# Four residual layers on one core: LayerNorm 1 kept by feature, its variance from a product with ones, its result added onto x in DRAM

## What is computed

```python
# layer 0, per token; D = 2 traces
ctx    = causal_ema(x, tau_ctx)
wg     = sigmoid([x, ctx] @ Wg.T + bg);  gated = x * wg
mod    = 0.5 + sigmoid(gelu(x @ Wn1.T + bn1) @ Wn2.T + bn2)
traces = causal_ema(gated * mod[d], tau[d])         # d = 0, 1
temporal = sum_d traces[d] * softmax(blend)[d]
gate   = sigmoid(temporal @ Wtemp.T + btemp)
soma   = gelu(x @ Wsoma.T + bsoma)
out    = (soma * gate) @ Wout.T
x = x + (out - mean(out)) / sqrt(var(out) + 1e-5) * gamma + beta   # LayerNorm 1
# layer 1: x = x + x @ W1[cat] + b1[cat]
# layer 2: h = relu(x @ A[lang] + a[lang]) @ B[lang] + b2[lang];  x = x + LayerNorm2(x + h)
# layer 3: x = x + x @ W3[subj].T + b3[subj]
```

## Time and profile before

| | |
|---|---|
| median of 3 runs | 786.71 us (786.17 to 790.17) |
| the profiled execution | 787.42 us |
| its span | 785.6 us |
| PE busy | 767.6 us (98%) |
| DVE busy | 533.8 us (68%) |
| ACT busy | 323.8 us (41%) |
| POOL busy | 101.4 us (13%) |
| HBM read, written | 40.67 MB, 25.20 MB |
| granted TensorE clock | full in every slice of the span |

### The profile page before, as it was taken

How to read it: one execution, slowest core, us unless ns; L and a number is a source line. 1 busy time by engine, 2 the same in 40 slices (tenths; PEclk the granted TensorE clock), 3 DMA queues, 4 the chain that set the end, 5 groups by cost and what they waited for, 6 DMA issues and landing times. The chain is left out here.

```text
span 785.6 us, 10804 instructions
## 1 busy us (share of the span) xinstructions
PE 767.6 (98%) x3628; PEld 628.3 (80%) x3628; DVE 533.8 (68%) x782; ACT 323.8 (41%) x525; POOL 101.4 (13%) x227
## 2 busy tenths in 40 slices
PE   5999999999999999999999999998999999999997
PEld 4888888888888888888888888776888888888885
DVE  3598894694695595595596587746775776657645
ACT  4444426226225315315325424656453544535332
POOL 2000020021012003003003004324001020110110
PEclk9999999999999999999999999999999999999999
DMA  7413004004004004102102514443142241313102
GB/s 222 167 55 108 27 1 161 28 0 161 27 0 160 27 0 146 41 0 111 76 0 81 136 53 157 146 146 141 41 148 70 105 147 41 121 63 111 40 28 82
DMA packets 32480, 66.29 MB, mean 84 GB/s; under 512 B 10800, under 2 KB 11824, under 8 KB 30400
## 3 DMA queue, kind: packets, MB, share of 16 engines
q1 hardware_dynamic: 32224, 65.87, 24.2%
q0 software_dynamic: 224, 0.00, 0.0%
HBM read 40.67 MB, written 25.20 MB: 84 GB/s over the span
## 5 line engine op out<-in xcount | busy, mean ns | idle before, releaser
L557 PE MATMUL pc<-x_h,wg_h 128*128 128x512 f32 x224 | 89.2, 398 | 0.0
L559 PE MATMUL pc<-x_h,wg_l 128*128 128x512 f32 x224 | 88.0, 393 | 0.0
L558 PE MATMUL pc<-x_l,wg_h 128*128 128x512 f32 x224 | 87.2, 389 | 0.0
L1292 DVE TENSOR_TENSOR_SCAN stage_b<-alpha,carry,stage_b 128x512 f32<-128x512 f32 x64 | 78.4, 1267 | 0.0
L999 ACT ACTIVATE ctx_t<-ctx_t,col_bg 128x512 f32<-128x512 f32 x32 | 23.2, 724 | 97.4 <-DVE ctx_t L1272 97.4
L1227 DVE TENSOR_TENSOR x_l<-x_t,x_h 128x512 fp32r<-128x512 f32 x32 | 22.2, 692 | 47.5 <-ACT x_t L949 47.5
L653 PE MATMUL pm<-t_h,wt_h 128*128 128x512 f32 x128 | 51.4, 402 | 0.0
L557 PE MATMUL pm<-wo_h,s_h 128*128 128x512 f32 x128 | 50.6, 395 | 0.7 <-DVE s_l L1251 0.7
L559 PE MATMUL pm<-wo_h,s_l 128*128 128x512 f32 x128 | 50.5, 394 | 0.0
L558 PE MATMUL pm<-wo_l,s_h 128*128 128x512 f32 x128 | 50.4, 394 | 0.0
L655 PE MATMUL pm<-t_h,wt_l 128*128 128x512 f32 x128 | 50.3, 393 | 0.0
(11 more groups left out here) (226 smaller groups left out, 1881.1 us busy)
## 6 DMA issues: line engine op xcount, KB each, us to landing
xt_scratch<-x_t SPq DMA_DIRECT2D x8, 1024.0 KB, 4.0
n_scratch<-stage_a SPq DMA_DIRECT2D x8, 1024.0 KB, 4.7
ctx_t<-xt_scratch SPq DMA_DIRECT2D x16, 512.0 KB, 6.4
x_tok<-in_x_dram SPq DMA_DIRECT2D x30, 256.0 KB, 2.8
out_dram<-x_tok SPq DMA_DIRECT2D x28, 256.0 KB, 2.0
s_h<-n_scratch SPq DMA_DIRECT2D x12, 512.0 KB, 4.9
mod<-mod_scratch SPq DMA_DIRECT2D x8, 512.0 KB, 3.5
stage_b<-in_L_cond_weight_dram SPq DMA_DIRECT2D x2, 1024.0 KB, 5.5
```

The costliest lines, as they stand in the source:

```text
L557: nc.tensor.matmul(acc, ah, bh, start=start and q == 0, stop=False)
L558: nc.tensor.matmul(acc, ah, bl, start=False, stop=False)
L559: last = nc.tensor.matmul(acc, al, bh, start=False, stop=stop and q == n - 1)
L1292: nc.vector.tensor_tensor_scan(tr[:, m % 2, :], alpha[:, 1 + d:2 + d].to_broadcast([P, BLK]), tr[:, m % 2, :], carry[:, D - d, m:m + 1], A ...
```

## The change

LayerNorm 1 is made by feature instead of by token, and its result is added onto x in DRAM.

- Wout is centred over its outputs when it is prepared: each turned quarter of it gets its row mean subtracted (centre_wout: bn_stats, bn_aggr and a negation on DVE; ACT's copy takes the negated mean as its bias, DVE's low part too). The mean of out over the features is then zero and is never computed. The factor 0.5 goes; the variance gets 4 * eps in its place.
- out_chunk(j, m) has Wout as weights and gives out by feature in pm[m].
- The variance over the features: ACT squares the four chunks into stage_a (square), DVE adds them up (add_squares, eps added in the last), ACT and DVE split the sum (squares_hi, squares_lo), PE multiplies it with a 128x128 matrix of 1/512 into pt[0] (variance, two matmuls), which gives the variance of each token on all partitions. DVE takes the reciprocal (inverse), ACT its root (root), and DVE's normalise1 makes gamma * out * rstd from pm[m] into stage_a.
- POOL's add_x1(j) issues one DMA with an add: stage_a onto block j of xt_scratch. store_n, the n loads, turn_y and y_sum_part are gone; load_y loads the sum, by feature. Blocks 2 and later wait for all eight of these stores.
- step_end alternates out_chunk(i-1, m) with v_chunk(i, m), puts variance(i-1) behind soma_chunk(i, 0), and the queues of ACT and DVE are ordered anew. norm1_scale leaves POOL.

```diff
+        ss_h, ss_l = h_h[:, :], h_l[:, :]
+        ones = c_h[:, NC - 1, 0:P]
+        rstd1 = gate[:, 0, :]
+        wo_mean = sb("wo_mean", [P, NC])
 ...
-            def store_n(j):
-                sp.wait_ge(ln_out, j * TILES + TILES)
-                sp.dma_start(block_of(n_scratch, j), stage_a[:, :, :]).then_inc(n_out, 16)
 ...
             def load_y(i):
 
-                sp.wait_ge(ty_done, i * NC)
-                sp.wait_ge(n_out, i * 16 + 16)
-                for half in range(2):
-                    load_n_half(i, s_h[:, 2 * half:2 * half + 2, :].bitcast(F32), half)
+                sp.wait_ge(x1_out, (i * 16 + 16) if isinstance(i, int) and i < 2 else NBLK * 16)
                 sp.wait_ge(y_lo, i * NC)
                 for half in range(2):
-                    load_xt_half(i, half)
+                    load_y_half(i, half)
 ...
+            def add_x1(j):
+
+                pool.wait_ge(xt_out, j * 16 + 16)
+                pool.wait_ge(ln_out, j * NC + NC)
+                pool.dma_start(block_of(xt_scratch, j), stage_a[:, :, :], accum_op=ALU.add).then_inc(x1_out, 16)
 ...
-                    norm1_scale(i - 1)
+                    add_x1(i - 1)
 ...
-            def out_product(j, k):
+            def out_chunk(j, m):
+                if m == 0:
                     pe.wait_ge(gate_t, j * NC + NC)
                     pe.wait_ge(s_hi, j * NC + NC)
                     pe.wait_ge(s_lo, j * NC + NC)
-                tok = out_cols(k)
-                product(pm[k][:, :], [(s_h[:, c, tok], s_l[:, c, tok], wo_h[:, c, :], wo_l[:, c, :])
+                o = out_cols(m)
+                product(pm[m][:, :], [(wo_h[:, c, o], wo_l[:, c, o], s_h[:, c, :], s_l[:, c, :])
                                       for c in range(NC)]).then_inc(wo_mm, 1)
 
+            def variance(j, bank_used):
+
+                pe.wait_ge(ss_hi, j + 1)
+                pe.wait_ge(ss_lo, j + 1)
+                pe.wait_ge(mod_raw, bank_used)
+                nc.tensor.matmul(pt[0][:, :], ones, ss_h, start=True, stop=False)
+                nc.tensor.matmul(pt[0][:, :], ones, ss_l, start=False, stop=True).then_inc(var_mm, 1)
+
             def step_end(i, first=False):
-                for m in range(NC):
-                    v_chunk(i, m)
                 if first:
+                    v_chunk(i, 0)
+                    v_chunk(i, 1)
                     ready(WOUT)
-                for k in range(TILES):
-                    out_product(i - 1, k)
-                for m in range(NC):
+                    out_chunk(i - 1, 0)
+                    v_chunk(i, 2)
+                    out_chunk(i - 1, 1)
+                    v_chunk(i, 3)
+                    out_chunk(i - 1, 2)
+                    out_chunk(i - 1, 3)
+                else:
+                    for m in range(NC):
+                        out_chunk(i - 1, m)
+                        v_chunk(i, m)
+                soma_chunk(i, 0)
+                variance(i - 1, i + 1)
+                for m in range(1, NC):
 ...
-            def turn_y(i, c, shared=False):
-
-                if c == 0:
-                    pe.wait_ge(yn_in, i * 32 + 32)
-                if c < 2 and shared:
-                    pe.wait_ge(x3_sum, i * NC + (c - 5))
-                if c >= 2:
-                    pe.wait_ge(y_sum, i * NC + (c - 1))
-                turn(pt[c % 2], [n_tile(i, k)[:, out_cols(c)] for k in range(TILES)]).then_inc(ty_done, 1)
 ...
+            temp_product(LAST, range(NC))
             pe.wait_ge(l1_hi, NC)
             pe.wait_ge(l1_lo, NC)
             pe.wait_ge(soma_g, NBLK * NC)
             l1_product(0, 0, 0)
             l1_product(0, 0, 1)
+            pe.wait_ge(mod_raw, NBLK)
+            pe.wait_ge(var_rec, LAST)
             turn_l3(0, 0, pt[0])
             turn_l3(0, 1, pt[1])
-            out_product(LAST, 0)
-            out_product(LAST, 1)
+            for m in range(NC):
+                out_chunk(LAST, m)
             turn_l3(0, 2, pt[0])
             turn_l3(0, 3, pt[1])
-            out_product(LAST, 2)
-            out_product(LAST, 3)
             l1_product(0, 0, 2)
+            pe.wait_ge(l3_hi, 3)
+            pe.wait_ge(l3_lo, 3)
+            variance(LAST, NBLK)
             l1_product(0, 0, 3)
             pe.wait_ge(l3_hi, NC)
             pe.wait_ge(l3_lo, NC)
-            turn_y(1, 0)
-            turn_y(1, 1)
             w1_product(0, 0)
-            turn_y(1, 2)
-            turn_y(1, 3)
-            pe.wait_ge(ln_out, NBLK * TILES)
+            pe.wait_ge(ln_out, NBLK * NC)
             for k in range(TILES):
                 xx_product(0, 0, k)
 ...
-                    nc.scalar.activation(hi, pm[c % 4][:, :], ACT.Identity, scale=W_SCALE[n]).then_inc(w_hi, 1)
+                    if n == WOUT:
+                        act.wait_ge(wo_stats, 2 * k + 2)
+                        nc.scalar.activation(hi, pm[c % 4][:, :], ACT.Identity,
+                                             bias=wo_mean[:, k:k + 1]).then_inc(w_hi, 1)
+                    else:
+                        nc.scalar.activation(hi, pm[c % 4][:, :], ACT.Identity).then_inc(w_hi, 1)
 ...
-            def normalise1(j, k):
-                if k == 0:
-                    act.wait_ge(ln_rstd, j + 1)
-                    after(act, n_out, j * 16)
-                nc.scalar.activation(stage_a[:, k, :], pm[k][:, :], ACT.Identity, bias=nbias[:, k:k + 1],
-                                     scale=rstd[:, k:k + 1]).then_inc(ln_out, 1)
+            def square(j, m):
+                act.wait_ge(wo_mm, j * NC + (m + 1))
+                if m == 0:
+                    after(act, x1_out, j * 16)
+                nc.scalar.activation(stage_a[:, m, :], pm[m][:, :], ACT.Square).then_inc(sq_done, 1)
+
+            def squares_hi(j, bank_used):
+                act.wait_ge(sq_sum, j * 3 + 3)
+                act.wait_ge(mod_mm, bank_used)
+                nc.scalar.activation(ss_h, stage_a[:, 0, :], ACT.Identity).then_inc(ss_hi, 1)
+
+            def root(j):
+                act.wait_ge(var_rec, j + 1)
+                nc.scalar.activation(rstd1, rstd1, ACT.Sqrt).then_inc(ln_rstd, 1)
 
             def traces_part(i, last=False):
+                square(i - 1, 0)
                 z_tanh(i, 0)
+                square(i - 1, 1)
                 z_tanh(i, 1)
+                temporal_hi(i, 0)
+                square(i - 1, 2)
                 z_tanh(i, 2)
-                temporal_hi(i, 0)
+                square(i - 1, 3)
+                temporal_hi(i, 1)
+                squares_hi(i - 1, i + 1)
                 z_tanh(i, 3)
-                temporal_hi(i, 1)
                 soma_gelu(i, 0)
+                root(i - 1)
                 soma_gelu(i, 1)
                 temporal_hi(i, 2)
-                normalise1(i - 1, 0)
 ...
+            def centre_wout(k):
+
+                c = W_BEFORE[WOUT] + k
+                dve.wait_ge(w_turned, c + 1)
+                nc.vector.bn_stats(stats[:, k, :], pm[c % 4][:, :]).then_inc(ln2_stats, 1)
+                dve.wait_ge(ln2_stats, k + 1)
+                nc.vector.bn_aggr(mv[:, k, :], stats[:, k, :]).then_inc(wo_stats, 1)
+                dve.wait_ge(wo_stats, 2 * k + 1)
+                nc.vector.tensor_scalar(wo_mean[:, k:k + 1], mv[:, k, 0:1], -1.0, None, ALU.mult).then_inc(wo_stats, 1)
 ...
-            def norm_stats(j, k):
-                dve.wait_ge(wo_mm, j * TILES + (k + 1))
-                nc.vector.bn_stats(stats[:, k, :], pm[k][:, :]).then_inc(ln_stats, 1)
-                dve.wait_ge(ln_stats, j * TILES + (k + 1))
-                dve.sem_inc(stats_seen, 1)
-                nc.vector.bn_aggr(mv[:, k, :], stats[:, k, :]).then_inc(ln_mv, 1)
+            def add_squares(j, m):
+
+                dve.wait_ge(sq_done, j * NC + (m + 1))
+                if m > 1:
+                    dve.wait_ge(sq_sum, j * 3 + (m - 1))
+                if m < NC - 1:
+                    nc.vector.tensor_tensor(stage_a[:, 0, :], stage_a[:, 0, :], stage_a[:, m, :],
+                                            ALU.add).then_inc(sq_sum, 1)
+                else:
+                    nc.vector.scalar_tensor_tensor(stage_a[:, 0, :], stage_a[:, 0, :], 4.0 * EPS * NC, stage_a[:, m, :],
+                                                   ALU.add, ALU.add).then_inc(sq_sum, 1)
+
+            def squares_lo(j):
+                dve.wait_ge(ss_hi, j + 1)
+                nc.vector.tensor_tensor(ss_l, stage_a[:, 0, :], f32(ss_h), ALU.subtract).then_inc(ss_lo, 1)
+
+            def inverse(j):
+                dve.wait_ge(var_mm, j + 1)
+                nc.vector.reciprocal(rstd1, pt[0][:, :]).then_inc(var_rec, 1)
+
+            def normalise1(j, m):
+                if m == 0:
+                    dve.wait_ge(ln_rstd, j + 1)
+                    dve.wait_ge(ss_lo, j + 1)
+                nc.vector.scalar_tensor_tensor(stage_a[:, m, :], pm[m][:, :], cols["gamma"][:, m:m + 1], rstd1,
+                                               ALU.mult, ALU.mult).then_inc(ln_out, 1)
```

(55 more changed lines are left out.)

152 lines of the change are left out of this document (49 added, 103 removed).

## The result

The changed kernel takes **834.11 us** (median of 4 runs, 830.97 to 837.58), the kernel before 787.16 in the same comparison: ratio 1.0586, 95% interval 1.056 to 1.0613 (the quotient of the two medians, 1.0596, lies inside it). The forecast was 804.4, with 793 to 814: slower was right, the size was not. Ratios here leave out a run more than 1.5% above the fastest of its own kernel, which was one run, 796.85 us, of the kernel with Wout uncentred. The profiled execution has a span of 831.6 us against 785.6, 46.0 more.

What follows compares the result with a forecast made beforehand. PE's back-to-back instructions were taken as the bound. 787.4 - 14.0 (turns) + 3.7 (variance matmuls) + 16.2 (variance waits) + 6.4 (Wout) + 2.4 (step 1) + 3.0 (passage) = 805.1, against the median 804.4 us; range 793 to 814.

Steps and rivals of the forecast that it cites:

- The wait at variance, 2.7 in each pass: First-stage loop: PE waits 2.7 us for DVE's squares_lo in each of passes 2 to 7, 16.2 us together.
- ready(WOUT), 6.4: Step 1: PE waits 6.4 us for Wout's centring, once; bounds 3.4 and 7.5.
- Step 1's variance, 2.4: Step 1: DVE's block work starts after the centring at 99.3, so PE waits 2.4 us more.
- RECIPROCAL, taken as 1.27: DVE's inverse: no row, so taken as long as the scan, 1.27 us; hidden inside the loop, not at the stage's end.
- 4.9 in the rival: Rival of a slow reciprocal: 8 passes of 0.6, 4.9 us, adding 7.2 at the last block; 811.6 us, chance 0.25.
- The loop covers 3.6 more: Slow-reciprocal rival, first-stage loop: its 3.6 us extra stays hidden there; only the last block pays.
- The margin of 13 against 19 us: Loop: temporal_lo(3) ends some 13 us after variance starts, while PE asks for it 19 us after.
- Table loads, nothing: ACT, two ACT_TABLE_LOADs of 1.28 us per root: cost nothing in the loop, as ACT idles 38 of 60 us.
- Passage, +3.0: Between the stages: later DVE, POOL's linear_lo and the variance chain add net 3.0 us, bounds 0 and 5.
- The rival on clock and store, 813 to 816 at 0.08: Loop: waits cost granted clock or the store holds square(0); half the passes lose 3 us more; 813 to 816, chance 0.08.
- The wait of 3.4 us was followed by matmuls at the old pace: Argument against the clock and store rival: the kernel before's 3.4 us PE wait did not slow the matmuls behind it.
- The store has 30 us: Argument against the clock and store rival: the next block's square(0) asks for the accumulating store's landing some 30 us later.

Runs made afterwards that it cites:

- the kernel with the variance later: Changed kernel with PE's variance moved one soma chunk later, behind soma_chunk(i, 1): 814.3 us, ratio 1.0332 against the kernel before.
- the one with the cheap inverse: Changed kernel with variance one soma chunk later and RECIPROCAL replaced by a multiplication by 1.0: 797.39 us, ratio 1.0111.
- the kernel with the 1.9 us waits: Kernel before the change plus only a PE wait behind soma_chunk(0) in passes 2 to 7, for a 32-byte transfer: 801.26 us, ratio 1.0171.
- the held and the plain store: Changed kernel with add_x1 held until the next block's last x tile landed: 826.77 us; changed kernel with that store not accumulating: 827.63 us.
- the longer wait alone: Kernel before plus only a PE wait behind soma_chunk(0), passes 2 to 7, its transfer issued behind soma_gelu(0), 0.8 us longer: 812.57 us, ratio 1.0321.
- the last three kernels: Variance later, Abs_reciprocal_sqrt on ScalarE, step 1 reordered around Wout: 794.09 us; plus two passage edits: 793.55; plus held store and step 1's squares reordered: 785.38.
- The last kernel: Kernel with step 1 reordered and two passage edits, plus add_x1 held and step 1's add_squares(1) and square(1) put later: 785.38 us, ratio 0.9968.

## Why the prediction was right and wrong

- **What bounds** (PE, so that every wait is paid in full): right. Each wait taken from the loop, or put into it, moved the time by about its length or by more.
- **Turns removed, 14.0.** A pass of the second stage between the same turns is 33.05 us before and 31.39 after, 1.66 less for the 1.75 taken. Right.
- **The wait at variance, 2.7 in each pass.** The view shows 2.7, and 2.9 from start to start; the way from gate_sum(0) to squares_lo took 21.7 us for the 21.86 summed. Right.
- **ready(WOUT), 6.4.** Measured 6.1. Right.
- **Step 1's variance, 2.4.** Measured 5.3. The step "the block's DVE work starts then" counted the loop's distances (and 21.6 of them, where the sum above it had 21.86). In step 1 ACT's tanh of gate_sum(0) stands behind square(0), which needs out_chunk(0), just started, and at half clock:

```profile
97.65 0.68 DVE L1267 TENSOR_TENSOR ctx_t<-pc,ctx_t 128x512 f32<-128x512 f32 x1
104.57 0.69 DVE L1271 SCALAR_TENSOR_TENSOR ctx_t<-ctx_t,x_t 128x512 f32<-128x512 f32 x1 [6.24 <-ACT ctx_t L972]
```

- **RECIPROCAL, taken as 1.27 with 0.67 below it; 4.9 in the rival (8 passes of 0.6 are 4.8).** Measured 3.35. By the Trainium skill (VectorE: DVE Perf Modes, First, the fixed hardware budget), with its repeat count of 8, the estimate was 4.3; the trace is between the two, nearer to the page. "The loop covers 3.6 more" was true only as long as PE waited at variance: the kernel with that wait removed pays 2.2 us a pass for it. The margin of 13 against 19 us was counted at the wrong place: temp_product was asked for its low part in time, but the copy of the x tile behind it in ACT's queue was not looked at.
- **Table loads, nothing.** Right: with the root an Identity the time is the same. The page (the Trainium skill, ScalarE: Activation LUTs, What ACT_TABLE_LOAD costs) adds a drain of about 1.4 us to each; here the activation starts 0.01 us behind its load:

```profile
394.83 1.28 ACT L959 ACT_TABLE_LOAD   x1
396.12 0.69 ACT L959 ACTIVATE soma<-pt,col_bsoma 128x512 f32<-128x512 f32 x1
```

- **Passage, +3.0** (0 to 5). The waits are +3.5. From the kernel with the variance later to the one with the cheap inverse, the wait for c_l goes from 2.7 to 0.2 and the one at the passage's head from 5.0 to 4.0.
- **The rival on clock and store, 813 to 816 at 0.08: this is the step that failed.** The forecast put the clock and the loads of x_tok at nothing. It was this rival's mechanism that came true, and both arguments against it were wrong. "The wait of 3.4 us was followed by matmuls at the old pace" took one event for a rule. What follows that wait in the profile of the kernel before, and then in that of the kernel with the 1.9 us waits, where the wait at the same place is 3.3:

```profile
540.10:543.50 3.40, 3.37 (x19) 2.99 (x20) 2.29 (x4) 1.80 (x4) 3.40 (x3) 1.00 0.02 5
```

```profile
552.20:555.60 3.40, 3.40 (x13) 3.00 (x14) 2.39 (x4) 1.80 (x4) 3.29 (x3) 0.54 0.02 5
```

  Of 24 waits of 2.5 to 2.8 us in the loop (the changed kernel, the held and the plain store, the longer wait alone), 22 are followed by a fall.

  "The store has 30 us" asked only who waits for the store, not which transfers its bytes lie in front of. And the rival was priced for half the loop only, at 3 us: the waits of step 1 and of the passage, and one wait for x_tok, bring falls as well, so the clock made up to 17 us and the loads 7.9. These two, with 2.9 in step 1, are 28 of the 30 us that were missed.

What stays open is when exactly the clock falls. The length of the wait alone does not decide. Two of the six waits at variance in the changed kernel were followed by no fall, while in the kernels with the held or the plain store all six were. The wait of 2.7 us at the variance of step 1, the same in six kernels that have the variance later, is followed by a fall in the profiles of four and not of two. And the 1.9 us that PE waits for Wout in the last three kernels is followed by one in every profile. The last kernel's:

```profile
97.00:100.40 3.40, 3.40 (x10) 2.68 (x9) 2.11 (x3) 0.00 (x0) 0.19 (x1) 0.55 0.00 0
```

## What to carry to other kernels

Where PE has no slack, a wait costs its length and can cost a fall of the clock on top, here 1.6 to 1.7 us. Behind waits of 1.9 us in an otherwise full loop that came once in six, behind waits of 2.5 to 2.8 nearly always. So count the fall in for a wait near 3 us, and hold it possible for a shorter one; that a single wait in a profile left the clock alone proves nothing. Of an added transfer ask what is issued just behind it, and how far apart the two engines that issue them are in time. A cost "hidden in the loop" may be hidden by the very wait one means to remove: price it again without that wait.

## What the runs showed of the hardware

- An accumulating store of 1 MB takes 8.6 us from issue to landing; the same tile, same queue, without accumulation 5.2.
- VectorE and GpSimd slow each other down. In the kernel with the root of the inverse on ScalarE, four of GpSimd's linear_lo take 6.5 us, 1.3 to 1.9 each, and VectorE's gate_soma beside them 1.6 to 1.8, where the kernel before has a mean of 0.72. The Trainium skill (GPSIMD Engine Reference, Specifications) says that the two share their way to SBUF; this trace agrees.

```profile
508.44 3.31 DVE L1241 SCALAR_TENSOR_TENSOR gate<-gate,soma 128x512 f32<-128x512 f32 x2 [1.36 <-ACT gate L937]
...
506.35 6.52 POOL L499 TENSOR_TENSOR wg_l<-x_t,wg_h 128x512 fp32r<-128x512 f32 x4 [2.62 <-ACT wg_h L1067]
```

- An activation of 128x512 with Abs_reciprocal_sqrt from PSUM takes 0.60 us, against 3.35 + 0.63 for reciprocal and root; its table loads are the same.
